# Last stage of a graph network with experts: expert outputs one step later, reciprocal roots on GpSimd, gate sums earlier, stores from SP's queue

## The chip, the cores and the metric

One core of one Trainium2 chip runs the whole program in one launch. The metric is the device time in microseconds (us) of that core, median over runs. Engines: PE is TensorE (PEld its weight loads), DVE is VectorE, ACT is ScalarE, POOL is GpSimd, SP is SyncE, which here only issues DMAs.

## The reference, cut to what matters

6250 nodes of 256 features, 206250 edges. An attention layer over the edges (all ahead of the last stage) leaves for every node a sum of weighted values and the sum of weights. What the last stage computes, for every node:

```python
out = weighted_values / (sum_of_weights + 1e-16)          # attention, by head
x_r = xn @ Wskip.T + bskip                                # xn: normalised x
beta = sigmoid(concat([out, x_r, out - x_r]) @ Wbeta.T)
h = beta * x_r + (1.0 - beta) * out
y = layernorm(xn + h, ln1_g, ln1_b)
t = layernorm(y + gelu(y @ W1.T + b1) @ W2.T + b2, ln2_g, ln2_b)
x2 = x + t
m = layernorm(x2)                                         # no gain, no bias
shared = relu(relu(m @ sW1 + sb1) @ sW2 + sb2) @ sW3 + sb3
expert[e] = relu(relu(m @ eW1[e] + eb1[e]) @ eW2[e] + eb2[e]) @ eW3[e] + eb3[e]   # 4 experts
gates = softmax(m @ gW + gb); w = softmax(top-2 of gates)
result = x2 + shared + sum(w[e] * expert[e])
```

All is float32. W1 is 256 to 1024, sW1 256 to 256, sW2 256 to 128, eW1 256 to 128, eW2 128 to 64, eW3 64 to 256.

## The kernel before, in words

Two stages come first and are not touched: normalisation with the key, value and query products, and the attention over the edges. The last stage begins at about 3006 us of the span. It works on the 49 blocks of 128 nodes in 13 parts (`parts`, `wd`): the first of 3 blocks, eleven of 4, the last of 2. Each engine has its own hand-written program, and they meet at semaphores only. Matrix operands are kept feature-major, so row tiles are transposed by TensorE (`transpose_rows`, L1440) into two buffers `tr`, and copied out by ScalarE (`transposed`, L1364). `r0` are the transposes of xn, `r1` of y, `r2` of m. Hidden layers (`hidden`, L1449 on TensorE, L1387 on ScalarE) go through two PSUM buffers `hid`: `w1` has 8 groups of four matmuls, `s1` 2, `e1` 4, `s2` 1, `e2` 4. Products that come out by node (`node_major`, L1456) go through three PSUM buffers `nat`: `skip` (two matmul pairs a block), `w2` (8 pairs a block) and `out` (one tile for the shared branch and one for each expert, so five tiles a block, each read by VectorE). A float32 product of 256 columns shows as two matmuls in the trace. For `nat` and `hid` a list `order` gives every tile its number; the same order must hold on the engine that fills and the one that empties.

A step s works on part s with W1 and W2 and on part c = s - 1 with the experts. TensorE's order in a step: W1(s), with the transposes of m(c) after its fifth group, gate logits (L1482), s1(c), W2(s), e1(c), s2(c), e2(c), transposes of y(s+1) and xn(s+2), expert outputs of c, skip(s+2).

VectorE's order in a step: `after_attention(s+1)` (gate sum L1236 to L1239, gate L1241 to L1245, first layer norm, y; L1256 is its last line), `gates(c)`, `divide_by_sum(s+2)` (L1215 to L1219), `add_ffn(s)` (L1264), `after_ffn(s)` (second and third layer norm; the last gives `mb`, which is m), `combine(c)` (L1323 and L1328, reading the output tiles), `skip_less_out(s+2)` (L1227). Every layer norm (`layernorm`) takes statistics (L1200), seven short operations (L37 to L43), waits for ScalarE's reciprocal root and scales (L1207).

ScalarE computes the root as exp(-0.5 ln(var + eps)) in `rstd`, L1376 and L1378, at three places of a step, and the gates' exponentials (L1369, L1382). Changing between these functions and gelu makes it load a table.

SP's queue loads weights, then for each step xn(s+3) and x(s+1); GpSimd's queue stores each part (L1170, L1173) once it is combined.

Of the kernel before, what the change touches and what calls it, by code (L numbers as in the profile page):

```python
# [24 lines left out]
ALU = mybir.AluOpType  # L25
ACT = mybir.ActivationFunctionType
AX = mybir.AxisListType

P = 128
# [16 lines left out]
def build(nc, a, out):  # L46
# [75 lines left out]
    with top:  # L122
# [877 lines left out]
        with ExitStack() as s3:  # L1000

            W = 4
# [42 lines left out]
            eps3 = sbt(s3, "eps3", [P, 1])  # L1047
# [5 lines left out]
            lv3 = sbt(s3, "lv3", [P, W])  # L1053
            rs3 = sbt(s3, "rs3", [P, W])
            zb = sbt(s3, "zb", [P, W])
# [33 lines left out]
            ws_landed, w3_landed, consts3, rows_set = sem("ws_landed"), sem("w3_landed"), sem("consts3"), sem("rows_set")  # L1089
# [10 lines left out]
            with nc.Block() as block:  # L1100
                @block.sync
                def _(sp):
# [39 lines left out]

                    for dst, src in loads[:NW3S]:
                        sp.dma_start(dst, src).then_inc(ws_landed, 16)
# [6 lines left out]
                    for s in range(NS):  # L1151
                        if s + 3 < NS:
                            load_xn(s + 3)
                        if s + 1 < NS:
                            load_x(s + 1)

                @block.gpsimd
                def _(pool):
                    pool.memset(tri[:, :, :], 1.0).then_inc(consts3, 1)
                    pool.wait_ge(consts3, 1)  # L1160

                    pool.affine_select(out=tri[:, :, :], in_=tri[:, :, :], compare_op=ALU.is_ge, fill=0.0, base=-1,
                                       pattern=[[1, NE], [-1, NE]], channel_multiplier=0).then_inc(consts3, 1)

                    for p, (t0, t1) in enumerate(parts):
                        pool.wait_ge(out_ready, p + 1)
                        whole = min(t1, N // P) - t0
                        last = min(t1 * P, N) - (t0 + whole) * P
                        if whole:
                            pool.dma_start(out[t0 * P:(t0 + whole) * P, :].rearrange("(j p) d -> p j d", p=P), accb[:, 0:whole, :]  # L1170
                                           ).then_inc(out_stored, 16)
                        if last:
                            pool.dma_start(out[(t0 + whole) * P:N, :], accb[0:last, whole, :]).then_inc(out_stored, 16)  # L1173
                    pool.wait_ge(out_stored, 16 * (NS - 1 + (whole > 0) + (last > 0)))

                @block.vector
                def _(dve):
                    ch = Chain(dve, "dve3")

                    dve.memset(eps3[:, :], LN_EPS).then_inc(rows_set, 1)  # L1180
# [17 lines left out]
                    def layernorm(dst, src, w):  # L1198
                        for j in range(w):
                            s = dve.bn_stats(st3[:, j, :], src[:, j, :])  # L1200
                        ch.step(s)
                        mean_and_var(dve, ch, st3[:, 0:w, :], mn3[:, 0:w], vr3[:, 0:w], D)
                        dve.sem_inc(var_ready, 1)
                        lns[0] += 1
                        dve.wait_ge(rstd_ready, 2 * lns[0])
# [24 lines left out]
                    def after_attention(p):  # L1230

                        w, d = wd[p], db[p % 3]
                        ob, x, t, y = weighted(p)[:, :, :, 0:C], xnb[p % 2], ta[:, 0:w, :], yb[:, 0:w, :]
# [5 lines left out]
                        dve.tensor_reduce(zb[:, 0:w], t, AX.X, ALU.add).then_inc(z_ready, 1)  # L1239
                        dve.wait_ge(ez_ready, p + 1)  # L1240
# [94 lines left out]
                    skip_less_out(0)  # L1335
                    after_attention(0)
                    divide_by_sum(1)
                    skip_less_out(1)
                    for s in range(NS + 1):
                        if s + 1 < NS:  # L1340
                            after_attention(s + 1)
                        if s >= 1:
                            gates(s - 1)
                        if s + 2 < NS:
                            divide_by_sum(s + 2)
                        if s < NS:
                            add_ffn(s)
                            after_ffn(s)
                        if s >= 1:
                            combine(s - 1)  # L1350
                        if s + 2 < NS:
                            skip_less_out(s + 2)

                @block.scalar
                def _(act):
                    act.wait_ge(rows_set, 2)
                    lns = [0]
# [13 lines left out]
                    def rstd(p):  # L1371

                        w = slice(0, wd[p])
                        lns[0] += 1
                        act.wait_ge(var_ready, lns[0])
                        act.activation(lv3[:, w], vr3[:, w], ACT.Ln, bias=eps3[:, 0:1]).then_inc(rstd_ready, 1)  # L1376
                        act.wait_ge(rstd_ready, 2 * lns[0] - 1)
                        act.activation(rs3[:, w], lv3[:, w], ACT.Exp, scale=-0.5).then_inc(rstd_ready, 1)  # L1378

# [9 lines left out]
                    transposed(0, 0)  # L1389
                    transposed(0, 1)  # L1390
                    exp_z(0)
                    rstd(0)
                    transposed(1, 0)
                    act.wait_ge(w3_landed, 16 * (NW3 - NW3S))
                    for s in range(NS + 1):
                        c = s - 1
                        if s < NS:
                            for k in range(KH):
                                hidden("w1", s, k, h1, ACT.Gelu, b1c)
                                if k == 2 and s + 1 < NS:  # L1400
                                    exp_z(s + 1)
                                if k == 4 and c >= 0:
                                    transposed(2, c)
                                if k == 5 and s + 1 < NS:
                                    rstd(s + 1)
                        elif c >= 0:
                            transposed(2, c)
                        if c >= 0:
                            for k in range(KD):
                                hidden("s1", c, k, sh1, ACT.Relu, sb1c)  # L1410
                            exp_gates(c, 0)
# [8 lines left out]
                        elif s < NS:  # L1420
                            rstd(s)
                        if s + 1 < NS:
                            transposed(1, s + 1)
                        if s + 2 < NS:
                            transposed(0, s + 2)
                        if s < NS:
                            rstd(s)

                @block.tensor
                def _(pe):  # L1430
                    pe.wait_ge(ws_landed, 16 * NW3S)
                    pe.wait_ge(rows_set, 2)
# [59 lines left out]
                    for s in range(NS + 1):  # L1492
                        c = s - 1
# [7 lines left out]
                        elif c >= 0:  # L1501
                            rows_of_m(c)
                        if c >= 0:
                            wc = wd[c] * P
                            gate_logits(c)
                            for k in range(KD):
                                hidden("s1", c, k, P, [(sW1[:, i, k * P:(k + 1) * P], rT[2][:, i, 0:wc]) for i in range(KD)])
                        if s < NS:
# [3 lines left out]
                        if c >= 0:  # L1512
# [7 lines left out]
                        if s + 1 < NS:  # L1520
                            rows_of_y(s + 1)
                        if s + 2 < NS:
                            rows_of_x(s + 2)
                        if c >= 0:
                            pe.wait_ge(hid_emptied, hid_at["e2", c] + NE)
                            for j in range(wd[c]):
                                cols, n = slice(j * P, (j + 1) * P), nat_at["out", c] + j * (1 + NE)
                                node_major(n, [(sh2[:, cols], sW3[:, :])])
                                for e in range(NE):
                                    node_major(n + 1 + e, [(e2[:, e, cols], eW3[:, e, :])])  # L1530
                        if s + 2 < NS:
                            skip(s + 2)
# [59 lines left out]
```

## Time and profile before

| what | value |
|---|---|
| median of 3 runs | 4067.2 us (4065.84 to 4069.83) |
| the profiled execution's own time | 4068.84 us |
| its span in the trace | 4067.0 us |
| mean granted clock of TensorE | 0.952 |
| busy over the span: TensorE, VectorE, ScalarE, GpSimd | 91%, 48%, 41%, 50% |

The profile is one execution recorded on the chip. Busy time is that of instructions at work; a wait is idle time with the engine or queue whose event ended it. The granted clock is given as a share of 2.4 GHz, so 0.50 is 1.2 GHz. The page cuts the span into 40 slices of about 102 us; the last stage fills slices 31 to 40. In the rows below, times are microseconds from the span's start.

### The profile page before, as it was taken

What the parts mean: (1) busy time and instruction counts of PE and PEld (TensorE: products, weight loads), DVE (VectorE), ACT (ScalarE), POOL (GpSimd) and SP (SyncE); (2) the same over time, 40 slices, a digit from 0 to 9 for tenths busy, and PEclk for the clock granted to TensorE, in tenths of its full rate; (3) what the DMA queues carried; (4) which work ended last, traced back from release to release, by engine and by line L of the source; (5) the groups of instructions that cost most, each with busy time, mean ns of one, the idle gap of its engine ahead of it and who ended that gap; (6) DMA issues with size and microseconds to landing.
All of it is one profiled execution on the core that took longest, in us unless ns stands there. A gap on an engine that the chain in (4) does not pass through costs nothing. (4 is left out here: it accounts for less than half of the span.)

```text
span 4067.0 us, 77637 instructions
## 1 busy us (share of the span) xinstructions
PE 3700.7 (91%) x22914; PEld 2352.3 (58%) x22914; DVE 1970.6 (48%) x5552; ACT 1681.0 (41%) x3636; POOL 2046.7 (50%) x2100
## 2 busy tenths in 40 slices
PE   5879999999999999999999999999967888888888
PEld 2346666666666666666666666666645555555555
DVE  5344444444444444444444444444446555555544
ACT  2134444444444444444444444444424343433442
POOL 3067777777777777777777777777720000000000
PEclk9989999999999999999999999999988888888887
DMA  6467677776777767777776777767740000000000
GB/s 200 156 164 186 181 184 184 189 186 183 185 185 186 187 184 187 186 185 189 187 190 183 185 188 186 182 183 190 188 105 21 15 26 16 21 16 22 13 13 13
DMA packets 637776, 572.41 MB, mean 141 GB/s; under 512 B 430486, under 2 KB 523991, under 8 KB 637700
## 3 DMA queue, kind: packets, MB, share of 16 engines
q0 software_dynamic: 159616, 429.57, 35.9%
q1 hardware_dynamic: 478100, 142.10, 16.8%
q8 instruction: 30, 0.49, 0.1%
q14 instruction: 30, 0.25, 0.0%
HBM read 632.99 MB, written 33.05 MB: 164 GB/s over the span
## 5 line engine op out<-in xcount | busy, mean ns | idle before, releaser
L610 POOL DMA_INDIRECT F<-kv_rows,srcg x1970 | 1994.7, 1013 | 841.2 <-issue 564.4
L688 DVE COPY PT<-pPT 128x384 f32<-128x384 f32 x393 | 219.0, 557 | 1164.9 <-PE pPT L878 1146.4
L885 PE MATMUL pZ<-F,PT 128*64 128x320 f32 x4704 | 743.1, 434 | 0.0
L858 PE MATMUL ring<-ident,F 128*128 128x128 f32 x3940 | 605.8, 285 | 120.6 <-ACT FT L790 111.9
L858 PEld LDWEIGHTS ring<-ident,F 128*128 128x128 f32 x3940 | 420.3, 141 | 406.4 <-ACT FT L790 203.9
L796 ACT ACTIVATE Pw<-pS,nMn 128x384 f32<-128x384 f32 x393 | 226.8, 577 | 954.5 <-DVE nMn L683 954.5
L790 ACT ACTIVATE FT<-ring 128x512 f32<-128x512 f32 (+1 forms) x1182 | 579.1, 525 | 73.4 <-PE ring L858 10.4
L1170 POOL DMA_DIRECT2D out_dram<-accb x13 | 9.7, 749 | 1047.1 <-DVEq L1332 1047.1
L885 PEld LDWEIGHTS pZ<-F,PT 128*64 128x64 f32 x4704 | 366.4, 136 | 254.5 <-issue 0.5
L867 PE MATMUL pS<-FT,qh 128*64 128x320 f32 x3144 | 512.0, 447 | 1.5 <-issue 1.1
L682 DVE TENSOR_REDUCE nmx<-pS 128x1 f32<-128x384 f32 x393 | 219.2, 558 | 202.1 <-PE pS L871 200.5
L867 PEld LDWEIGHTS pS<-FT,qh 128*64 128x64 f32 x3144 | 191.2, 136 | 157.9 <-issue 2.5
L871 PE MATMUL pS<-F,G 80*64 80x320 f32 x1572 | 279.7, 433 | 0.0
L834 ACT ACTIVATE Zs<-pZ 128x320 f32<-128x320 f32 x392 | 171.6, 438 | 185.3 <-PE pZ L885 185.3
L1456 PE MATMUL nat<-eW,e 65*128 65x256 f32 x392 | 168.0, 598 | 63.2 <-DVE accb L1323 63.2
L676 DVE TENSOR_SCALAR F<-F,nid 16x640 f32<-16x640 int32 x394 | 214.4, 544 | 19.2 <-issue 1.3
L898 PE MATMUL pZv<-ident,Zs 128*128 128x64 f32 x1568 | 218.2, 262 | 0.0
L878 PE MATMUL pPT<-ident,Pw 128*128 128x128 f32 x1179 | 215.3, 291 | 1.1 <-ACT Pw L796 1.1
L891 PE MATMUL pM<-ident,F 64*128 64x64 f32 x1965 | 206.6, 233 | 0.0
L898 PEld LDWEIGHTS pZv<-ident,Zs 128*128 128x128 f32 x1568 | 205.9, 192 | 0.0
L808 ACT ACTIVATE G<-pM 64x512 f32<-64x512 f32 x99 | 58.5, 591 | 352.4 <-PE pM L848 352.4
L891 PEld LDWEIGHTS pM<-ident,F 64*128 64x128 f32 x1965 | 153.0, 139 | 66.2 <-issue 66.2
(215 smaller groups left out, 4458.0 us busy)
## 6 DMA issues: line engine op xcount, KB each, us to landing
F<-in_edge_attrT SPq DMA_DIRECT2D x788, 80.0 KB
F<-kv_rows,srcg POOLq DMA_INDIRECT x1970
F<-in_dst SPq DMA_DIRECT2D x788, 20.0 KB
srci<-src_front SPq DMA_DIRECT2D x796, 1.5 KB, 3.5
kv_rows<-kvs SPq DMA_DIRECT2D x7, 1792.0 KB, 6.7
qb<-q_cols SPq DMA_DIRECT2D x100, 64.0 KB, 2.9
U<-in_x SPq DMA_DIRECT2D x7, 896.0 KB, 10.9
xn_rows<-xs SPq DMA_DIRECT2D x7, 896.0 KB, 6.7
```

Of the source, the lines that this page charges most:

```text
L610: pool.indirect_dma_start(out=F[s][:, t, 0:KV], out_offset=None, in_=kv_d, in_offset=bass.IndirectOffsetOnAxis(ap=srcg[j % GB][:, col:col ...
L682: ch.step(dve.tensor_reduce(nmx[:, j:j + 1], pS[:, 0:SW], AX.X, ALU.max, negate=True))
L688: dve.tensor_copy(PT[:, :, :], pPT[:, 0:SW].rearrange("p (t r) -> p t r", r=P)).then_inc(pt_emptied, 1)
L790: act.activation(FT[j % 2][:, :, t0 * P:t1 * P], ring[n % 2][:, 0:KD * w].rearrange("p (k e) -> p k e", e=w), ACT.Copy).then_inc(ring_empt ...
L796: act.activation(Pw[:, :], pS[:, 0:SW], ACT.Exp, bias=nMn[:, j:j + 1], accum_out=lsum[:, j:j + 1]).then_inc(p_done, 1)
L858: m = pe.transpose(ring[n % 2][:, k * w + (t - t0) * P:k * w + (t - t0 + 1) * P], F[j][:, t, k * P:(k + 1) * P], ident[:, :])
L867: pe.matmul(pS[o * HP:(o + 1) * HP, o * HP:o * HP + OW], qh[half][:, c, g + o, :, :].rearrange("p c r -> p (c r)"), FT[j % 2][:, c, o * OW ...
L871: m = pe.matmul(pS[o * HP:(o + 1) * HP, o * HP:o * HP + OW], G3[half][0:K3, g + o, :, :].rearrange("p c r -> p (c r)"), F3[s][0:K3, o * OW ...
L878: m = pe.transpose(pPT[:, t * P:(t + 1) * P], Pw[:, t * P:(t + 1) * P], ident[:, :])
L885: m = pe.matmul(pZ[rows, 0:ZW], PT[:, t, rows], F[s][:, o * TO + t, D:FP], start=(t == 0), stop=(t == KB - 1))
L891: m = pe.transpose(pM[:, t * DE:(t + 1) * DE], F3[s][0:DE, t * P:(t + 1) * P], ident[0:DE, 0:DE])
L898: pe.matmul(pZv[:, g].rearrange("p (o c r) -> p o c r", o=2, c=KD)[:, :, c, :], Zs[:, c * P:(c + 1) * P], ident[:, :].rearrange("p (o c r) ...
```

## The change

Four things change, all in the last stage.

- The expert outputs and `combine` of a part move one step later. TensorE's order in a step becomes: W1(s) with the transposes of m(s-1), expert outputs of s - 2, gate logits and s1(s-1), transposes of y(s+1) and xn(s+2), W2(s), skip(s+2), e1, s2, e2(s-1). There is one step more, and `order` follows.
- The reciprocal root becomes one power, (var + eps) to -0.5, on GpSimd, with eps added by VectorE. GpSimd sets a constant of -0.5 at the start.
- The gate's wide sum (`gate_sum`) leaves `after_attention(p)` and runs two steps earlier in VectorE's text, after `skip_less_out(p)` in the step before; the exponential for it comes at the end of ScalarE's step.
- The stores are issued from SP's queue.

```diff
-            for s in range(NS + 1):
-                order += [("w1", s), ("r2", s - 1), ("s1", s - 1), ("w2", s), ("e1", s - 1), ("s2", s - 1), ("e2", s - 1),
-                          ("r1", s + 1), ("r0", s + 2), ("out", s - 1), ("skip", s + 2)]
+            for s in range(NS + 2):
+                order += [("w1", s), ("r2", s - 1), ("out", s - 2), ("s1", s - 1), ("r1", s + 1), ("r0", s + 2), ("w2", s),
+                          ("skip", s + 2), ("e1", s - 1), ("s2", s - 1), ("e2", s - 1)]
...
                 @block.sync
-                    for s in range(NS):
+                    for s in range(NS + 2):
                         if s + 3 < NS:
                             load_xn(s + 3)
+                        if s >= 2:
+                            store(s - 2)
                         if s + 1 < NS:
                             load_x(s + 1)
+                    sp.wait_ge(out_stored, 16 * stored[0])
...
                 @block.gpsimd
+                    pool.memset(half[:, :], -0.5).then_inc(half_set, 1)
...
+                    def rstd(p):
+                        lns[0] += 1
+                        pool.wait_ge(var_ready, lns[0])
+                        pool.tensor_tensor(rs3[:, 0:wd[p]], vr3[:, 0:wd[p]], half[:, 0:wd[p]], ALU.pow).then_inc(rstd_ready, 1)
...
                 @block.vector
+                        ch.step(dve.tensor_scalar(vr3[:, 0:w], vr3[:, 0:w], LN_EPS, None, ALU.add))
                         dve.sem_inc(var_ready, 1)
...
-                    for s in range(NS + 1):
+                    for s in range(NS + 2):
                         if s + 1 < NS:
                             after_attention(s + 1)
-                        if s >= 1:
+                        if s >= 2:
+                            combine(s - 2)
+                        if 1 <= s <= NS:
                             gates(s - 1)
                         if s + 2 < NS:
                             divide_by_sum(s + 2)
                         if s < NS:
                             add_ffn(s)
-                            after_ffn(s)
-                        if s >= 1:
-                            combine(s - 1)
                         if s + 2 < NS:
                             skip_less_out(s + 2)
+                            gate_sum(s + 2)
+                        if s < NS:
+                            after_ffn(s)
...
                 @block.scalar
-                                if k == 2 and s + 1 < NS:
-                                    exp_z(s + 1)
-                                if k == 5 and s + 1 < NS:
-                                    rstd(s + 1)
...
+                        if s + 1 < NS:
+                            transposed(1, s + 1)
+                        if s + 2 < NS:
+                            transposed(0, s + 2)
                         if c >= 0:
                             exp_gates(c, 0)
                             exp_gates(c, 1)
                             for e in range(NE):
                                 hidden("e1", c, e, e1, ACT.Relu, eb1c)
-                                if e == 1 and s < NS:
-                                    rstd(s)
                             hidden("s2", c, 0, sh2[:, None, :], ACT.Relu, sb2c)
                             for e in range(NE):
                                 hidden("e2", c, e, e2, ACT.Relu, eb2c, EH2)
...
+                            exp_z(s + 2)
...
                 @block.tensor
-                    for s in range(NS + 1):
-                        c = s - 1
+                    for s in range(NS + 2):
+                        c, o = s - 1, s - 2
...
+                        if o >= 0:
+                            pe.wait_ge(hid_emptied, hid_at["e2", o] + NE)
+                            for j in range(wd[o]):
+                                cols, n = slice(j * P, (j + 1) * P), nat_at["out", o] + j * (1 + NE)
+                                node_major(n, [(sh2[:, cols], sW3[:, :])])
+                                for e in range(NE):
+                                    node_major(n + 1 + e, [(e2[:, e, cols], eW3[:, e, :])])
```

## Rows read from the trace of the kernel before

**Rows 1.** Busy time by stretch: PE, PEld, DVE, ACT, POOL, PEclk, DMA share, GB/s.
```profile
3647.60:3729.60 82.00, 72.28 (x229) 45.85 (x229) 47.70 (x115) 32.59 (x51) 0.75 (x1) 0.85 0.06 20
```
**Rows 2.** Chain of waits that ended last: start us, us, what.
```profile
3155.47 1.39 DVE mb L1207 x4
...
3808.35 1.39 DVE mb L1207 x4
...
3889.36 1.39 DVE mb L1207 x4
...
3965.55 1.39 DVE mb L1207 x4
```
**Rows 3.** Timeline of PE: start us, us, engine line op, shapes, count [idle before <-releaser].
```profile
3565.74 2.08 PE L1456 MATMUL nat<-eW,e 65*128 65x256 f32 x4 [5.43 <-DVE accb L1323]
...
3585.55 8.75 PE L1449 MATMUL hid<-rT,W1T 128*128 128x512 f32 x20
...
3604.34 5.35 PE L1449 MATMUL hid<-rT,sW 128*128 128x512 f32 x8 [0.79 <-ACT h L1387]
3609.53 13.98 PE L1456 MATMUL nat<-W2T,h 128*128 128x256 f32 x64
...
3631.51 1.96 PE L1449 MATMUL hid<-sh,sW 128*128 128x512 f32 x4 [1.14 <-ACT e L1387]
...
3637.22 0.66 PE L1440 MATMUL tr<-ident,yb 128*128 128x128 f32 x4
...
3640.22 0.71 PE L1440 MATMUL tr<-ident,xnb 128*128 128x128 f32 x4 [0.26 <-ACT rT L1364]
```
**Rows 4.** Busy time in stretches of 2 us, columns as in rows 1.
```profile
3563.70:3565.70 2.00, 0.00 (x0) 0.00 (x0) 1.91 (x3) 0.15 (x1) 0.00 (x0) 0.50 0.00 0
...
3577.70:3579.70 2.00, 2.00 (x6) 1.55 (x6) 0.97 (x2) 0.00 (x0) 0.00 (x0) 0.50 0.00 0
...
3605.70:3607.70 2.00, 2.00 (x3) 0.67 (x2) 1.93 (x3) 0.00 (x0) 0.00 (x0) 0.50 0.00 0
```
**Rows 5.** Timeline of DVE, first step and a full step, columns as in rows 3.
```profile
3096.24 1.06 DVE L1207 TENSOR_SCALAR mb<-tb,mn,rs 128x256 f32<-128x256 f32 x3 [1.94 <-ACT rs L1378]
...
3586.20 1.22 DVE L1236 TENSOR_TENSOR ta<-U,w 128x1024 f32<-128x1024 f32 x1
...
3593.14 0.17 DVE L1241 TENSOR_SCALAR ezb<-ezb 128x4 f32<-128x4 f32 x1 [1.93 <-ACT ezb L1369]
...
3602.33 1.38 DVE L1207 TENSOR_SCALAR db<-ta,mn,rs 128x256 f32<-128x256 f32 x4 [2.89 <-ACT rs L1378]
...
3607.52 0.17 DVE L1286 TENSOR_TENSOR g<-pg,rows 128x16 f32<-128x16 f32 x1
...
3624.00 1.41 DVE L1200 BATCH_NORM_STATS2 st<-tb 128x6 f32<-128x256 f32 x4
...
3630.83 1.38 DVE L1207 TENSOR_SCALAR db<-tb,mn,rs 128x256 f32<-128x256 f32 x4 [4.02 <-ACT rs L1378]
...
3644.51 1.38 DVE L1207 TENSOR_SCALAR mb<-tb,mn,rs 128x256 f32<-128x256 f32 x4 [5.57 <-ACT rs L1378]
```
**Rows 6.** Timeline of POOL in the first stage, columns as in rows 3.
```profile
59.87 4.52 POOL L283 TENSOR_SCALAR_AFFINE_SELECT selh<-selh 128x4 f32<-128x4 f32 x14
...
91.26 1.64 POOL L315 MEMSET U<- 128x1848 f32 x1 [3.79 <-DVE xs L354]
```
**Rows 7.** Timelines of PE and DVE at the end, columns as in rows 3.
```profile
4025.34 2.08 PE L1456 MATMUL nat<-eW,e 65*128 65x256 f32 x4 [3.52 <-DVE accb L1323]
...
4041.54 1.87 PE L1482 MATMUL pg<-gW,rT 128*128 128x4 f32 x8 [0.47 <-ACT rT L1364]
...
4046.82 2.49 PE L1449 MATMUL hid<-rT,eW 128*128 128x256 f32 x8
...
4057.90 2.04 DVE L1328 SCALAR_TENSOR_TENSOR accb<-nat,we,accb 128x256 f32<-128x256 f32 x4
```
**Rows 8.** DMA issues of the last stage: count, KB each, median us to landing.
```profile
out_dram<-accb POOLq DMA_DIRECT2D x11, 512.0 KB, 3.3
```

More of the change, by code:

```diff
@@ L1052, in build @@
             vr3 = sbt(s3, "vr3", [P, W])
-            lv3 = sbt(s3, "lv3", [P, W])
             rs3 = sbt(s3, "rs3", [P, W])
+            half = sbt(s3, "half", [P, W])
             zb = sbt(s3, "zb", [P, W])
@@ L1141, in load_x, with store @@
                         sp.dma_start(xb[:, 0:t1 - t0, :], x_d[:, t0:t1, :]).then_inc(xb_landed, 16)
+                    stored = [0]
+                    def store(p):
+                        t0, t1 = parts[p]
+                        sp.wait_ge(out_ready, p + 1)
+                        whole = min(t1, N // P) - t0
+                        last = min(t1 * P, N) - (t0 + whole) * P
+                        if whole:
+                            stored[0] += 1
+                            sp.dma_start(out[t0 * P:(t0 + whole) * P, :].rearrange("(j p) d -> p j d", p=P), accb[:, 0:whole, :]
+                                         ).then_inc(out_stored, 16)
+                        if last:
+                            stored[0] += 1
+                            sp.dma_start(out[(t0 + whole) * P:N, :], accb[0:last, whole, :]).then_inc(out_stored, 16)
                     for dst, src in loads[:NW3S]:
@@ L1160, in _ @@
                     pool.wait_ge(consts3, 1)
+                    pool.memset(half[:, :], -0.5).then_inc(half_set, 1)
+                    pool.wait_ge(half_set, 1)
                     pool.affine_select(out=tri[:, :, :], in_=tri[:, :, :], compare_op=ALU.is_ge, fill=0.0, base=-1,
                                        pattern=[[1, NE], [-1, NE]], channel_multiplier=0).then_inc(consts3, 1)
[L1165 to L1174, printed above, removed]
+                    lns = [0]
+                    def rstd(p):
+                        lns[0] += 1
+                        pool.wait_ge(var_ready, lns[0])
+                        pool.tensor_tensor(rs3[:, 0:wd[p]], vr3[:, 0:wd[p]], half[:, 0:wd[p]], ALU.pow).then_inc(rstd_ready, 1)
+                    rstd(0)
+                    for s in range(NS):
+                        if s + 1 < NS:
+                            rstd(s + 1)
+                        rstd(s)
+                        rstd(s)
                 @block.vector
@@ L1239, in after_attention @@
                         dve.tensor_reduce(zb[:, 0:w], t, AX.X, ALU.add).then_inc(z_ready, 1)
+                        dve.wait_ge(z_ready, p + 1)
+                    def after_attention(p):
+                        w, d = wd[p], db[p % 3]
+                        ob, x, t, y = weighted(p)[:, :, :, 0:C], xnb[p % 2], ta[:, 0:w, :], yb[:, 0:w, :]
                         dve.wait_ge(ez_ready, p + 1)
@@ L1335, in _ @@
                     skip_less_out(0)
+                    gate_sum(0)
                     after_attention(0)
@@ L1511, in _ @@
                                 node_major(nat_at["w2", s] + j, [(h1[:, k, j * P:(j + 1) * P], W2T[:, k, :]) for k in range(KH)])
-                        if c >= 0:
+                        if s + 2 < NS:
+                            skip(s + 2)
+                        if 0 <= c < NS:
                             for e in range(NE):
@@ L1519, in _ @@
                                 hidden("e2", c, e, EH2, [(eW2[:, e, :], e1[:, e, 0:wc])])
[L1520 to L1532, printed above, removed]
 NW3, NW3S = 26, 10
```

47 lines of the change are left out of this document (19 added, 28 removed).

## The prediction

> **What bounds the kernel now.** I read the page first: TensorE is the only engine near full, and slices 31 to 40, the last stage, differ from the rest: GpSimd idles and TensorE's clock drops. Only that stage is changed; I price nothing ahead of 3010 us. Next came the busy times by stretch. One step (a part of four blocks) takes 82 us: TensorE 72.3 us busy at a mean granted clock of 0.85, VectorE 47.7, ScalarE 32.6 [rows 1]. No engine is full; order and clock set the step. The chain of waits shows the ring. I mark a part c by its "mb", the last normalisation (call its end M(c)): M(1) = 3156.9, M(9) = 3809.7, so (3809.7 - 3156.9)/8 = 81.6 us a part; M(10) = 3890.7, M(11) = 3966.9 [rows 2]. TensorE's timeline has the holes. After the first tiles of "out" it stands 5.43 us, until VectorE has finished mb and can combine; two more holes are 0.79 us and 1.14 us, behind ScalarE [rows 3]. The fine stretches give the larger cost: after the hole the clock is 0.50 (1.2 GHz) and stays there through all expert outputs, with TensorE busy 2.00 of 2.00 us; it is 0.50 once more behind the gate logits [rows 4]. Expert outputs and skip thus take 19.8 us (3565.74 to 3585.55) [rows 3]. VectorE waits 2.89, 4.02 and 5.57 us for ScalarE's reciprocal roots [rows 5].
>
> **The change, part by part.**
> *Roots on GpSimd.* Log, exponential and their table loads leave ScalarE; VectorE gets one small addition (0.20 us with its gap, like its neighbours), GpSimd one power of 128x4, called p with both hand-offs. The trace has no power on GpSimd. Below: a chained small selection, 14 in 4.52 us, 0.32 us each; above: its longest computing row, 1.64 us for 128x1848 [rows 6]. The operand has four columns, so I take a value near the low end, p = 0.6, and keep both. Three a part.
> The Trainium skill ("GPSIMD Engine Reference", 4.1 Engine selection) speaks against the move: elementwise work belongs on VectorE, GpSimd being about twice as slow on two inputs. No row tests that; it would put p at an estimated 0.4 us and change the sum by some 8 us.
>
> *Gate sums early.* The four wide passes move from ahead of the gate's exponential to behind skip's subtraction, in the previous step. They are 5.0 us (3586.20 to 3593.14 less the wait of 1.93) [rows 5], still on VectorE's way, now ahead of mb instead of behind it; the wait for that exponential goes.
>
> *Expert outputs a step later.* Combine(s-2) now stands behind after_attention(s+1), and outputs(s-2) behind W1(s). Does VectorE come to it before TensorE? Count both from the end of skip. TensorE: e1, 16 matmuls at 0.43 us (20 in 8.75) = 6.9; s2 and e2, 3631.51 to 3637.22 = 5.7; W1's first five groups 8.6; rows_of_m 2.0 (four tiles through two buffers, my estimate); W1's last 12 matmuls 5.2; three output tiles (as many as there are buffers) 1.3 [rows 3]. Sum 29.7 us.
> VectorE: last subtraction 0.7; gate sum 5.0; after_ffn up to mb, 2.8 + 0.2 + p + 8.1 + 0.2 + p + 1.4 = 12.7 + 2p (3624.00 to 3630.83 less 4.02; 3630.83 to 3644.51 less 5.57; mb itself) [rows 5]; bias addition 1.26; after_attention without its sum, 6.3 + 0.2 + p + 5.2 = 11.7 + p (3593.14 to 3602.33 less 2.89; 3602.33 to 3607.52) [rows 5]; first release 0.45. Sum 31.8 + 3p = 33.6. **So TensorE still waits, about 4 us**, at the same door. In this trace holes of 5.43 and 3.52 us were followed by half clock, those of 1.14 and 0.79 us in themselves were not [rows 3, 7]. I expect the clock to fall again, and outputs never raised it [rows 4].
>
> *The new ring.* mb, bias 1.26, after_attention 11.7 + p, outputs 0.45 + 17 tiles at 0.854 (two matmuls of 0.43 each at half clock; VectorE needs only 0.51 a tile, four in 2.04 [rows 7]) = 14.9, gate logits at half clock 3.7 (eight take 1.87 [rows 7]), s1 partly at half clock 6.0 (between 5.35 [rows 3] and 8 x 0.86), transposes of y and x 3.6 (3637.22 to 3640.9, [rows 3]), W2 13.8, skip 3.5 (a quarter of W2's matmuls), subtraction 0.7, gate sum 5.0, after_ffn 12.7 + 2p: 76.9 + 3p = **78.7 us** against 81.6 on average before [rows 2]. The rest of TensorE (e1, s2, e2, W1) lies beside VectorE; if that cover were gone it would cost the 1.6 us between 21.2 (TensorE's arrival at rows_of_m) and 18.4 + 2p (mb).
>
> *First steps.* Ahead of M(0) come transposes 3.6, skip 3.5, 0.7 and gate sum 5.0, less about 7 us of root and exponential waits: M(0) = 3097.3 [rows 5] + 6 = 3103. M(1): 1.3 + 10.5 + p + 3.6 + 13.8 + 3.5 + 0.7 + 5.0 + 12.7 + 2p = 53, so 3156, as before. M(2): ring less five tiles, 74.4. M(9) = 3156 + 74.4 + 7 x 78.7 = 3781, 28 us early. M(10): skip, gate sum and transposes of a two-block part, 4.8 less, 73.9: 3855, 36 early.
> *Last steps.* Here the new order has least against it. M(11): no skip, no gate sum, a short after_attention (9.3 with p), so the hole shrinks to about 1 us and the clock should hold: 9.3 + 8.6 + 1.8 + 5.4 + 1.0 + 13.8 + 0.7 + 13.9 = 54, against 76.2 (bias and after_attention; outputs at VectorE's pace; logits; s1; transposes of y; W2; subtraction; after_ffn). M(12): TensorE sets it, 2.3 + 1.9 + 2.6 + 9.6 + 1.8 + 4.4 + 6.9 + 0.7 + 9.5 = 40 (its lateness at rows_of_m, those transposes, W1's rest on two blocks, outputs, logits, s1, W2 on two blocks, subtraction, after_ffn on two blocks). From M(12) to the end 37: 2.4 more of e1 to e2 of part 11, transposes 1.0, outputs 9.6, logits 1.5, s1 2.5, and from part 12's e1 to the end as before, 4046.8 to 4067.0, 20.2 [rows 7]. That is 77 against 4067.0 - 3966.9 = 100. End 3855 + 54 + 77 = 3986, **81 us early**.
>
> *Stores from SP's queue.* 14 DMAs move. SP's order is next x-norm load, store, next x load; the load behind the store waits for x_used anyway, set later in the same step than out_ready, and combine of the next part asks for the store a step later. Cost nothing; if that cover were gone, one transfer, 3.3 us, a step [rows 8]. The final store stays behind the last combine.
>
> The profiled execution took 4068.8 us for a span of 4067.0, 1.6 us above the median of 4067.2. 4068.8 - 81 = 3988, less 1.6: **3986 us**. Anything within 0.2% (8 us) of 4067 counts as the same, about what measurements of this kernel tell apart.
>
> **Rivals.**
> 1. *The clock holds.* If the hole is nearer 2 us, outputs go at VectorE's pace: 0.45 + 8.2 instead of 14.9, logits 1.8 instead of 3.7, s1 3.5 to 5.4 instead of 6.0. The ring falls to about 68 to 70 us, 9.5 less, nine times: some 85 us, **3900 us**. For: ScalarE's two smaller holes go, and my 4 us is a difference of two sums near 30 that an error of 2 us would halve. Against: 31.8 - 29.7 leaves 2.1 us even at p = 0. Also in this case: the clock falls but rises during the outputs. The Trainium skill ("TensorE: Matmul & The Clock Gate", What's actually happening) says that busy stretches release the throttle. The trace disagrees for these matmuls of 65 rows: busy throughout at 0.50, without a rise [rows 4]. Chance 0.24.
> 2. *Slower: the power is dear.* 39 powers (13 x 3) stand one behind another on VectorE's way, so the time is 3986 + 39 (p - 0.6). It passes 4067 at p = 2.7; at p = 3.5 it is **4099 us**. For: no power in the trace, and each is a wait of VectorE with everything queued behind it. Against: the two bounds [rows 6]. Chance 0.07 of being slower; between p = 1.6 and 2.7 (4025 to 4067) another 0.05.
> 3. *Only the ring gains.* The last two stretches gain 22 and 23 us by my sum; if each hides a wait that I have not seen, and the clock falls there too, nearly all of it goes: **4030 us**. For: no full step precedes them, so their clock is the least certain. Chance 0.12.
> 4. *The change doesn't do what it says*: outputs wait for mb through VectorE's order all the same and the removed root waits come back elsewhere: **4067**. Chance 0.02.
>
> **How the numbers follow.** Forecast 0.50 for 3986, its own range 3960 to 4020. The range reaches down over rival 1 (3895) and up to part of rival 3 (4038), leaving out 0.15 to 0.2. Faster 0.91, same 0.02, slower 0.07.
>
> **What the profile after would show.** ScalarE's loads fall to two a step, roots gone; GpSimd shows 39 powers: their mean is the first thing to read. A step of 78 to 79 us; a hole of about 4 us before an output tile, ended by VectorE's accb, and 0.50 behind it until s1; M(11) - M(10) near 54. I am wrong if the hole is under 2 us or outputs run at 1.00 (rival 1), if VectorE's idle before L1207 exceeds 1.6 us (rival 2), or if TensorE waits for m instead.

## The result, and the profile after

The changed kernel took 3996.40 us (median of 3 runs, 3996.38 to 3996.52) against 4067.2 us: a ratio of 0.9825, 95% interval 0.9803 to 0.9847, 71 us off. 3986 us was predicted, with 3895 to 4038 as its range. In a later comparison it took 3999.59 us against 4066.54 us (0.9837, 0.9823 to 0.985).

In the profiled execution (span 3994.6 us) TensorE's last product of line 913, after which the last stage follows, starts at 3000.4 us, and at 3004.3 us in the profile before. I therefore also give the **last stage**, the span less that start: 1062.7 us before, 994.2 us after, a gain of 68.5 us. Where a time below is set beside one that the prediction forecast, 3.9 us are added to it.

First the chain of waits that ended last, over one part (start us, us, what), to be read against [rows 2]:

```profile
3643.79 0.44 DVE accb L1353
3644.27 14.87 PE nat L1473 x34
3659.14 3.21 PE pg L1499 x16
3662.35 5.40 PE hid L1466 x8
...
3671.38 17.28 PE nat L1473 x80
...
3692.93 1.23 DVE zb L1263
...
3697.33 1.02 POOL rs L1191
3698.38 1.39 DVE db L1231 x4
...
3706.84 1.02 POOL rs L1191
3707.88 1.39 DVE mb L1231 x4
...
3717.20 1.01 POOL rs L1191
3718.24 1.39 DVE db L1231 x4
```

This is the ring that the prediction drew: expert outputs, logits, s1, transposes, W2 with skip, gate sum, the LayerNorms, and round again, with three powers on it. TensorE's timeline of the same part, against [rows 3]:

```profile
3636.94 0.59 PE L1473 MATMUL nat<-sW,sh 128*128 128x256 f32 x2
3637.37 1.03 PE L1473 MATMUL nat<-eW,e 65*128 65x256 f32 x4
3644.27 2.07 PE L1473 MATMUL nat<-eW,e 65*128 65x256 f32 x4 [5.87 <-DVE accb L1353]
...
3651.26 3.62 PE L1473 MATMUL nat<-eW,e 65*128 65x256 f32 x8
...
3658.94 3.41 PE L1499 MATMUL pg<-gW,rT 128*128 128x4 f32 x16
3662.21 5.53 PE L1466 MATMUL hid<-rT,sW 128*128 128x512 f32 x8
```

Three output tiles go out at 1.03 us for four matmuls, then TensorE stands 5.87 us for VectorE's first release, and the same four matmuls take twice as long. The fine stretches, against [rows 4] (columns as in rows 1):

```profile
3642.00:3644.00 2.00, 0.00 (x0) 0.00 (x0) 1.93 (x3) 0.00 (x0) 0.00 (x0) 0.51 0.00 0
...
3650.00:3652.00 2.00, 2.00 (x6) 1.64 (x5) 1.26 (x3) 0.00 (x0) 0.00 (x0) 0.50 0.00 0
3662.00:3664.00 2.00, 2.00 (x4) 1.02 (x5) 0.52 (x3) 0.00 (x0) 0.00 (x0) 0.50 0.13 46
3672.00:3674.00 2.00, 2.00 (x11) 1.77 (x10) 0.53 (x4) 1.32 (x2) 0.00 (x0) 1.00 0.00 0
```

The granted clock is 0.50 (1.2 GHz) from the hole on into s1, with TensorE busy 2.00 of 2.00 us once the hole is over, and 1.00 in W2. VectorE's timeline shows why the release is late, against [rows 5]:

```profile
3628.23 1.38 DVE L1231 TENSOR_SCALAR mb<-tb,mn,rs 128x256 f32<-128x256 f32 x4 [1.18 <-POOL rs L1191]
...
3638.60 1.38 DVE L1231 TENSOR_SCALAR db<-ta,mn,rs 128x256 f32<-128x256 f32 x4 [1.18 <-POOL rs L1191]
...
3643.79 0.42 DVE L1353 TENSOR_TENSOR accb<-nat,tb 128x256 f32<-128x256 f32 x1
```

Attention's LayerNorm and y of the next part stand between mb and the first release. VectorE waits 1.18 us for each root in place of 2.89, 4.02 and 5.57 us. One row of the page has the powers:

```profile
L1191 POOL TENSOR_TENSOR rs<-vr,half 128x4 f32<-128x4 f32 (+2 forms) x39 | 37.9, 972 | 916.4 <-DVEq L1227 916.4
```

The end differs from the ring in the last parts. Ahead of the outputs shown next, VectorE has only the short attention of the two-block part to do, and after that none. TensorE's timeline there, the counterpart of [rows 7]:

```profile
3874.76 2.00 PE L1473 MATMUL nat<-eW,e 65*128 65x256 f32 x8
...
3883.83 1.84 PE L1499 MATMUL pg<-gW,rT 128*128 128x4 f32 x16
3885.54 3.68 PE L1466 MATMUL hid<-rT,sW 128*128 128x512 f32 x8
```

Without a hole ahead of them, eight output matmuls take 2.0 us, the logits 1.84 and s1 3.68, where the ring pays 3.62, 3.41 and 5.53.

### The profile page after: what moved, and what is told of

It reads as the page before. It is cut to its first block and busy times, and to the rows that moved or that the text cites. A ratio compares the mean times of both kernels' runs of the same rounds, so it can differ in the third digit from the quotient of the medians.

```text
span 3994.6 us, 77537 instructions
## 1 busy us (share of the span) xinstructions
PE 3671.7 (92%) x22914; PEld 2332.8 (58%) x22914; DVE 1977.5 (50%) x5590; ACT 1519.0 (38%) x3445; POOL 2073.7 (52%) x2126
## 5 line engine op out<-in xcount | busy, mean ns | idle before, releaser
L790 ACT ACTIVATE FT<-ring 128x512 f32<-128x512 f32 (+1 forms) x1182 | 578.8, 525 | 73.6 <-PE ring L858 10.4
L1191 POOL TENSOR_TENSOR rs<-vr,half 128x4 f32<-128x4 f32 (+2 forms) x39 | 37.9, 972 | 916.4 <-DVEq L1227 916.4
L1473 PE MATMUL nat<-eW,e 65*128 65x256 f32 x392 | 150.7, 547 | 51.8 <-DVE accb L1353 51.8
```

The source lines that it names most:

```text
L790: act.activation(FT[j % 2][:, :, t0 * P:t1 * P], ring[n % 2][:, 0:KD * w].rearrange("p (k e) -> p k e", e=w), ACT.Copy).then_inc(ring_empt ...
L1473: m = pe.matmul(nat[n % NATS][:, 0:D], l, r, start=(q == 0), stop=(q == len(terms) - 1))
```

## The experiments

Theory: the time of a part is set by the ring through VectorE, three powers long; TensorE's hole in it costs its own length and then the clock behind it. The question that the result left: are 71 us what the moved roots bring, or a rest of it, with the order of the outputs taking something back? Rivals: the reorder is the gain and the roots a detail; or the hole is harmless and the clock falls for another reason.

### Each half of the change alone

**Roots only**: the kernel before, with the roots as powers on GpSimd, everything else in its old place.

```diff
-                        dve.wait_ge(rstd_ready, 2 * lns[0])
+                        dve.wait_ge(rstd_ready, lns[0])
...
+                    def rstd(p):
+                        lns[0] += 1
+                        pool.wait_ge(var_ready, lns[0])
+                        pool.tensor_tensor(rs3[:, 0:wd[p]], vr3[:, 0:wd[p]], half[:, 0:wd[p]], ALU.pow).then_inc(rstd_ready, 1)
```

> The kernel before with its reciprocal roots alone moved to GpSimd; order of work, gate sums and stores stay as they were. Theory (the root waits kept VectorE late for the first output tile): from the end of W2, VectorE needs 0.6 + 12.7 + 2.4 + 1.3 + 0.4 = 17.4 us to its first release, TensorE 6.9 + 5.7 + 3.6 + 1.3 = 17.5 to the third tile, so the hole of 5.4 us closes, the clock stays at 1.00 and the outputs go at VectorE's 0.51 us a tile: a step of 67 to 70 us against 81.9, the whole near 3930 us, faster than the changed kernel. Rival 1 (the gain of the change is its order): the step falls only by the two root waits on the way to mb, about 7 us, the clock still drops: near 3990. Rival 2 (root waits lie beside other work): 4060 to 4067.

**Order only**: the changed kernel, with logarithm and exponential for the roots back on ScalarE, after W1's third and eighth groups and after e1. Other places for them on ScalarE were not tried, so its time holds for these places.

```diff
-                        pool.tensor_tensor(rs3[:, 0:wd[p]], vr3[:, 0:wd[p]], half[:, 0:wd[p]], ALU.pow).then_inc(rstd_ready, 1)
...
+                        act.activation(lv3[:, w], vr3[:, w], ACT.Ln, bias=eps3[:, 0:1]).then_inc(rstd_ready, 1)
+                        act.wait_ge(rstd_ready, 2 * lns[0] - 1)
+                        act.activation(rs3[:, w], lv3[:, w], ACT.Exp, scale=-0.5).then_inc(rstd_ready, 1)
```

> The changed kernel with its roots back on ScalarE (logarithm and exponential), placed after W1's third group, after its eighth and after e1; order, gate sums and stores as changed. Theory: every root costs 3.1 to 4 us instead of GpSimd's 1.4 with the added eps, all on the way of mb: a step of 86 to 90 us against 80.2, the steps lose against the kernel before and the last two parts gain, 4060 to 4110 us. Rival (the order is what brings the gain): at most 4010 us.

Measured on one chip, the kernel before at 4066.89 us (the changed kernel's time is that of the first comparison, beside 4067.2):

| | outputs as before | outputs a step later |
|---|---|---|
| roots on ScalarE | 4066.9 us | 4144.9 us (ratio 1.0187, 1.017 to 1.0204) |
| roots on GpSimd | 3882.7 us (0.9549, 0.9533 to 0.9565) | 3996.4 us (the changed kernel) |

The roots bring 184 us by themselves; the new order (with early gate sums and SP's stores) costs 78 us with slow roots and 114 us with fast ones (116 us on one chip, in the last table). The first came out 47 us below what was expected, the second 35 us above the range given: both expectations took the cost of the order too low. TensorE's timeline with the roots alone moved:

```profile
3591.99 0.60 PE L1455 MATMUL nat<-sW,sh 128*128 128x256 f32 x2
3592.42 2.24 PE L1455 MATMUL nat<-eW,e 65*128 65x256 f32 x8
...
3601.79 3.69 PE L1455 MATMUL nat<-WskT,rT 128*128 128x256 f32 x16
...
3615.78 0.71 PE L1439 MATMUL tr<-ident,mb 128*128 128x128 f32 x4 [1.28 <-ACT rT L1381]
```

and its busy time over one step (columns as in rows 1):

```profile
3568.90:3633.50 64.60, 62.32 (x230) 37.88 (x229) 47.91 (x117) 22.41 (x38) 3.84 (x4) 1.00 0.07 21
```

No hole ahead of the outputs, the clock at 1.00 throughout, and TensorE busy 62.32 of 64.60 us: a step is 17 us shorter than the 81.6 before. The reason lies in rows shown already. VectorE's root waits fall from 12.48 us to about 3.5, some 9 us less, and the hole that these waits caused was 5.43 us; so VectorE now comes to its combine in time. This holds for the steps of the ring; the clock falls once more near the end (see "Beyond both kernels"). With the order alone VectorE waits 4.76, 5.07 and 2.42 us for roots:

```profile
3705.19 1.38 DVE L1220 TENSOR_SCALAR mb<-tb,mn,rs 128x256 f32<-128x256 f32 x4 [4.76 <-ACT rs L1401]
3719.23 1.38 DVE L1220 TENSOR_SCALAR db<-ta,mn,rs 128x256 f32<-128x256 f32 x4 [5.07 <-ACT rs L1401]
...
3781.06 1.38 DVE L1220 TENSOR_SCALAR db<-tb,mn,rs 128x256 f32<-128x256 f32 x4 [2.42 <-ACT rs L1401]
3793.93 1.38 DVE L1220 TENSOR_SCALAR mb<-tb,mn,rs 128x256 f32<-128x256 f32 x4 [4.76 <-ACT rs L1401]
```

The step is 3793.93 - 3705.19 = 88.7 us, 8.4 above the 80.3 of the changed kernel (mean of seven steps); the waits are 12.25 - 3.54 = 8.7 us longer. In the new order nearly every microsecond of a root is on the ring.

### Each power twice

```diff
+                        pool.tensor_tensor(rs2[:, 0:wd[p]], vr3[:, 0:wd[p]], half[:, 0:wd[p]], ALU.pow)
                         pool.tensor_tensor(rs3[:, 0:wd[p]], vr3[:, 0:wd[p]], half[:, 0:wd[p]], ALU.pow).then_inc(rstd_ready, 1)
```

> The changed kernel with every power taken twice on GpSimd (the first into a tile that nobody reads). Theory (39 powers one behind another on VectorE's way): 39 times 1.0 us more, 4035 us, a step 3.0 us longer. Rival (the power is hidden, or the step is pinned by the clock): 3996 to 4010 us.

Measured: 4037.62 us (0.9929, 0.9912 to 0.9946), 41 us above the changed kernel. The last stages, 1031.6 and 994.2 us, differ by 37.4, or 0.96 for each of 39 powers: about a power's length, but not evenly. Each of VectorE's waits grows by 0.97 us, and the step from 80.3 to 82.8, so 2.5 us for three (3.0 expected). From M(10) to M(11) (M as in the prediction, the end of a part's mb) it is 65.4 us against 54.2, since a hole opens where the changed kernel has none, and the outputs behind it run at half speed:

```profile
3908.31 1.82 PE L1475 MATMUL nat<-eW,e 65*128 65x256 f32 x4 [1.76 <-DVE accb L1355]
...
3910.78 3.62 PE L1475 MATMUL nat<-eW,e 65*128 65x256 f32 x8
```

From M(11) to the end it is 3.7 us less. So the roots of a part lie almost wholly on the ring, and the agreement of the total with 39 full powers is in part luck.

### The hole filled with useless work

Twelve products that nobody reads, on TensorE ahead of the expert outputs of a part (of ten parts in the changed kernel), and the same in the kernel before (eleven parts):

```diff
+                        if o >= 0 and s + 1 < NS:
+                            for _ in range(12):
+                                pe.matmul(pg[:, 2 * P:4 * P], W2T[:, 0, 0:P], W2T[:, 1, 0:D], start=True, stop=True)
```

> The changed kernel, with 12 products of 128x256 (W2 by itself, written to an unused part of the gate logits' bank, read by nobody) put on TensorE ahead of each part's expert outputs, 5.2 us of useless work in a hole of 5.9 us. Theory (the hole drops the clock, the dropped clock costs 10 us a step): the outputs run at 1.00, a tile each 0.51 us, a step of 70 us against 80.2, about 3910 us, faster with more work. Rival (outputs are slow for another reason: their 65 rows, VectorE, the buffers): 3996 us, or later by what the filler overruns.

> The kernel before, with 12 products of 128x256 that nobody reads on TensorE ahead of a part's expert outputs, where it waits in every part of the ring. Nothing else is changed. Theory: what the wait costs is mostly the granted clock behind it (outputs, pg and logits at 0.50); with TensorE kept busy in the wait the clock holds, and a part takes some 73 to 74 us in place of 82: about 3965 us (3940 to 4000). Rival: the wait is what costs, the clock follows from something else: 4067 us or, with the products' own 1.5 us in each part, up to 4085 us.

Measured for the changed kernel with it: 3932.07 us (0.9665, 0.9648 to 0.9681). The step falls from 80.3 to 71.53 us. TensorE's timeline and the busy times by stretch show why:

```profile
3603.03 1.22 PE L1473 MATMUL nat<-eW,e 65*128 65x256 f32 x4 [0.66 <-DVE accb L1353]
```

```profile
3587.00:3658.53 71.53, 69.10 (x253) 43.09 (x252) 47.90 (x116) 19.86 (x36) 3.02 (x3) 0.98 0.07 23
...
3610.00:3612.00 2.00, 2.00 (x14) 1.77 (x14) 1.86 (x5) 0.00 (x0) 0.00 (x0) 1.00 0.00 0
```

VectorE is as late as before (from the end of mb to the matmul that it releases it is 14.7 us in both), but TensorE has worked until then, and the outputs run at 1.00. So of what the hole costs a part, 8.8 us are the clock behind it; the wait itself is still there, as useless work. The step was expected 1.5 us shorter and the time 22 us shorter (3910): s1 still takes 5.38 us in place of 3.68, since the clock is 0.50 again behind the logits (3615 to 3617 us).

The kernel before with the same products ran with three others on a second chip, on which the kernel before itself took 4753.19 us. The attention stage is slower there (the last product of line 913 starts at 3672 to 3704 us), while the last stage is not: one and the same kernel (roots and gate's exponential on GpSimd, below) has a last stage of 865.0 us there and of 863.9 us on another chip. I compare last stages. With the products it is 4670.8 - 3703.6 = 967.2 us against 1062.7, 95 us shorter (84 us by the medians on that chip, ratio 0.9821, 0.9791 to 0.9852), 73.1 us a step on average:

```profile
4289.96:4364.00 74.04, 69.57 (x254) 42.98 (x253) 47.40 (x113) 32.57 (x52) 0.75 (x1) 0.98 0.07 22
4364.00:4436.36 72.36, 67.89 (x254) 42.41 (x253) 47.41 (x114) 32.58 (x52) 0.75 (x1) 1.00 0.06 19
```

Useless products alone give the kernel before more than the 68.5 us that the change gives in the last stage. The wait's own length was the smaller part of its price, in both kernels.

### The order on VectorE, and the old places restored

**Combine first**: in the changed kernel VectorE takes the combine of part s-2 ahead of attention's LayerNorm of part s+1.

```diff
-                        if s + 1 < NS:
-                            after_attention(s + 1)
                         if s >= 2:
                             combine(s - 2)
+                        if s + 1 < NS:
+                            after_attention(s + 1)
```

> The changed kernel with one move on VectorE: the combine of part s-2 is issued ahead of the attention's LayerNorm and y of part s+1. Theory: TensorE's wait ahead of the expert outputs (5.87 us) goes, since it is for VectorE's adds that queue behind that LayerNorm; in its place TensorE waits for y behind the skip product, some 7 us, with the clock falling there; about 73 us for a part and 3930 us. Rival: the new wait costs as much as the old, 80 us for a part, 3996 us or more.

Measured: ratio 0.9742 (0.9717 to 0.9767), last stage 4608.3 - 3672.0 = 936.3 us, 58 less than the changed kernel's, 72.9 us a step. The hole has moved, as expected:

```profile
4218.21 2.28 PE L1457 MATMUL tr<-ident,yb 128*128 128x128 f32 x8 [7.37 <-DVE yb L1284]
```

It is longer than the old one (7.37 against 5.87 us) and yet costs less, since what follows it is 16 transposes and W2 in place of thirty-odd output matmuls, sixteen logits and s1: W2's 64 matmuls take 14.10 us, against 13.98 in the changed kernel, so the clock is back by then. The clock over a step is 0.93 to 0.95, against 0.83 and 0.85.

**Old places**: the changed kernel with outputs, skip, combine and the transposes of y and xn where they were (and the gate's exponential back behind W1's third group); roots on GpSimd, gate sum early and stores from SP's queue stay.

```diff
-            for s in range(NS + 2):
-                order += [("w1", s), ("r2", s - 1), ("out", s - 2), ("s1", s - 1), ("r1", s + 1), ("r0", s + 2), ("w2", s),
-                          ("skip", s + 2), ("e1", s - 1), ("s2", s - 1), ("e2", s - 1)]
+            for s in range(NS + 1):
+                order += [("w1", s), ("r2", s - 1), ("s1", s - 1), ("w2", s), ("e1", s - 1), ("s2", s - 1), ("e2", s - 1),
+                          ("r1", s + 1), ("r0", s + 2), ("out", s - 1), ("skip", s + 2)]
```

> The changed kernel, but with the expert outputs, the skip product and VectorE's combine back in the places that they had before (outputs of a part behind its own W2, ahead of the next y and W1); the roots stay one power on GpSimd, the gate sum stays right behind the LayerNorm, and the stores stay on SP's queue. Theory: the whole loss against the kernel with the roots alone moved (3882.7 us) is the order of the outputs, and gate sums and SP's stores are worth nothing: 3883 us, within 10, a part of the ring each 64.6 us, TensorE's clock at 1.00. Rival: the early gate sum puts itself ahead of VectorE's work for y or for the combine, or SP's stores hold the loads: 3900 to 3990 us.

Measured: ratio 0.9613 (0.959 to 0.9636) on the second chip, last stage 874.5 us, 64.59 us a step, as with the roots alone. The new place of the outputs, with what moved along with it, is thus the whole of the loss. Early gate sums and SP's stores make 3 us at most, between 877.4 and 874.5, and not evenly: up to M(0) it is 4.7 us more than with the roots alone, from M(10) to M(11) 7.6 us less (62.9 against 70.5), where with the roots alone the clock falls, as shown below. The first of these was not looked into.

### Beyond both kernels

**Roots and the gate's exponential on GpSimd**, in the kernel before (w12 and w23 with their signs turned, so that zb is -z):

```diff
-                    def exp_z(p):
-                        act.wait_ge(z_ready, p + 1)
-                        act.activation(ezb[:, 0:wd[p]], zb[:, 0:wd[p]], ACT.Exp, scale=-1.0).then_inc(ez_ready, 1)
+                    def exp_z(p):
+                        pool.wait_ge(z_ready, p + 1)
+                        pool.tensor_tensor(ezb[:, 0:wd[p]], ec3[:, 0:wd[p]], zb[:, 0:wd[p]], ALU.pow).then_inc(ez_ready, 1)
```

> The kernel before with its roots on GpSimd (as in the run with the roots alone), and the gate's exponential made on GpSimd too, as e to the power of -z, so that ScalarE loads no table in the ring at all. The order of the outputs is that of before. Theory: the 1.28 us that TensorE still waits for ScalarE's rows of the transposes in each part goes, as ScalarE's two remaining loads were in its way: 63.2 to 63.6 us in place of 64.6 for each part, 3865 us (3855 to 3876). Rival: the wait has another releaser and stays, or GpSimd's power of the gate comes later than ScalarE's exponential did: 3883 us or somewhat above.

Measured on the second chip: ratio 0.9598 (0.9557 to 0.9639), last stage 865.0 us, 63.93 us a step. The expectation said that ScalarE then loads no table at all; that was careless, as the exponentials of the expert gates stay there. Loads fall from four a part to two. The last comparison put the versions side by side on a chip like the first, together with one that has all parts of the change but the new place of the outputs, and the gate's exponential on GpSimd:

> The changed kernel unaltered, beside the next three on one chip. Theory and rival alike: from TensorE's last product of line 913 to the end 994 us as in its first profile; the total follows from how long the stage before lasts on this chip: 3996 us, or some 4670 us where the granted clock of the attention stage is about 0.9.

> The kernel before with its roots on GpSimd and nothing else, unaltered, on the same chip as the changed kernel. Theory: 117 us less than the changed kernel from the last product of line 913 to the end (877 us), and some 114 us less in all: the order of the outputs costs that. Rival: the two chips so far differed, and the distance is smaller than 80 us.

> The kernel before with roots and the gate's exponential on GpSimd, unaltered. Theory: 0.65 us less for each part than with the roots alone, 12 us less in all: the ratio to it 0.997. Rival: no difference, since the wait for the rows of the transposes is made up elsewhere.

> The changed kernel with the outputs back in the places that they had before, and the gate's exponential on GpSimd as well as the roots; gate sum early, stores on SP's queue. Theory: what the parts give adds up: 3 us for the early start of the first part, 12 us for the gate's exponential: 862 us behind the last product of line 913, some 15 us less in all than with the roots alone. Rival: with the gate sum early its power on GpSimd stands in front of nothing, and the gain is that of the exponential alone, 865 us.

| | median of 5, us | ratio, 95% interval | last stage, us |
|---|---|---|---|
| changed kernel | 3999.59 | 0.9837, 0.9823 to 0.985 | 993.9 |
| roots alone | 3883.82 | 0.9549, 0.9536 to 0.9562 | 878.3 |
| roots and gate's exponential | 3871.05 | 0.9522, 0.9509 to 0.9535 | 863.9 |
| all parts, outputs in their old place | 3869.42 | 0.9513, 0.95 to 0.9526 | 864.4 |

(The kernel before: 4066.54, median of 9.) TensorE's waits in the last stage, in all, times and longest, first with the roots alone, then with the gate's exponential moved as well:

```profile
PE tr L1439 <- ACT rT L1381: 25.2, 45, 1.3
PE nat L1455 <- DVE db L1245: 23.9, 2, 15.0
PE tr L1439 <- DMA xnb<-xn_rows: 16.0, 1, 16.0
```

```profile
PE nat L1458 <- DVE db L1255: 24.6, 2, 15.7
PE tr L1442 <- ACT rT L1391: 17.9, 45, 0.6
PE tr L1442 <- DMA xnb<-xn_rows: 15.9, 1, 15.9
```

The longest wait for ScalarE's rows falls from 1.3 to 0.6 us, all of them from 25.2 to 17.9, and the time by 12.8 us, 12 expected. That the total agrees is luck. The last stage is 14.4 us shorter, and of that the parts from M(1) to M(10) give 5.0 (64.6 against 63.9 a step), while 8.3 lie between M(10) and M(11), 70.5 against 62.2. There the clock falls with the roots alone and holds with the exponential moved, behind holes of the same length (first the former, then the latter):

```profile
3728.06 1.22 PE L1455 MATMUL nat<-eW,e 65*128 65x256 f32 x4 [0.96 <-DVE accb L1341]
...
3729.74 3.66 PE L1455 MATMUL nat<-eW,e 65*128 65x256 f32 x8
```

```profile
3721.27 1.22 PE L1458 MATMUL nat<-eW,e 65*128 65x256 f32 x4 [0.96 <-DVE accb L1351]
...
3722.85 2.07 PE L1458 MATMUL nat<-eW,e 65*128 65x256 f32 x8
```

Why it falls in one of them stays open.

The two fastest can't be told apart: 1.6 us, intervals that overlap, last stages of 863.9 and 864.4; the 3 us that the early gate sum was thought to add are not seen. "ScalarE: Activation LUTs" of the Trainium skill (What ACT_TABLE_LOAD costs) puts a switch at 1.28 us of load and 1.38 of drain; the changed kernel's trace agrees on the load, but shows no drain: the instruction ahead of the load ends at 3671.80 us, and the one behind it comes at once:

```profile
3671.82 1.28 ACT L1406 ACT_TABLE_LOAD   x1
3673.12 0.21 ACT L1406 ACTIVATE gx<-g 128x16 f32<-128x16 f32 x1
```

What is left of waits in these two is mostly single long ones: 15.9 us for an x-norm load, and two for skip differences, 24.6 us in all.

## Why the prediction was right, and what it missed

**The forecast case happened, by its mechanism.** The order of the race at the outputs was counted as 31.8 + 3p against 29.7 us from the end of skip. Skip ends 79.65 us (a step) ahead of 3688.66, at 3609.0: VectorE's release comes 35.3 us later, TensorE 29.4 us later. The clock fell behind the hole and stayed down through the outputs; rivals 1 (it holds), 3 (only the ring gains) and 4 didn't happen.

**The term that was mis-sized is p.** "A value near the low end, p = 0.6": the trace has 1.18 us from the end of VectorE's addition to the normalisation, of which 1.01 is the power itself. By the prediction's own sums, 31.8 + 3 x 1.18 - 29.7 = 5.6 us of hole (measured 5.87, forecast about 4), and 76.9 + 3 x 1.18 = 80.4 us of ring (measured 80.3 on average from M(2) to M(9), forecast 78.7). The nearest-row argument failed: a selection on few columns says little of a power on few columns. The bounds of 0.3 and 1.6 us held. Doubling the powers showed the slope, 0.96 us on average for each of 39, so that rival 2 was a matter of size alone.

**The sum by stretches.** Two rows of the chain of waits give M(1) and M(9), with the length of mb and 3.9 us added:

```profile
3151.48 1.39 DVE mb L1231 x4
...
3788.65 1.39 DVE mb L1231 x4
```

M(0) was forecast at 3103 and came at 3102.7, M(1) at 3156 and 3156.8; here the dearer p was made up by other terms of the start. Eight steps later M(9) came at 3793.9, 12.9 us behind the forecast 3781, and 8 x 3 x 0.58 = 13.9. From there on the delay stays: M(10) is 75 us further (forecast 74), M(11) 54 (54), M(12) 39 (40), the end 37 (37). "Here the new order has least against it" held: no hole, outputs at 1.00. Of the ring's terms the outputs were exact (14.87 against 14.9), the logits a little high (3.2 against 3.7), s1 right on average (5.4 us in this part and 6.5 in the one before it, against 6.0), W2 and skip 17.28 against 17.3.

The last stage thus ended 12.5 us later than forecast, and the time came out 10.4 us later, 3996.4 against 3986: the stages ahead, which the change doesn't touch, happened to be 3.9 us shorter in this run, while the 1.6 us that the prediction took off, because the profiled execution of the kernel before was that much above its median, had no counterpart here. The gain that was priced at 81 us is 68.5. The formula of rival 2, 3986 + 39 (p - 0.6), gives 4009 with p = 1.18, too much: of the 39 powers the 24 from M(1) to M(9) show in the end.

**The side terms.** Two loads a part, as forecast. The gate sum of a part runs one step earlier than before, as the prediction has it (the description of the change says two). Stores from SP's queue and early gate sums were costed at nothing beyond what the ring already holds; with the outputs restored to their old place neither is seen in the time.

**The rule on engine selection** of the Trainium skill ("GPSIMD Engine Reference", 4.1 Engine selection), which gives elementwise adds, products and maxima to VectorE, points the wrong way for this operation in this place: GpSimd takes 1.01 us where VectorE's neighbouring operations (not powers) take 0.17, more than twice as slow, and yet the move is the whole gain, since it replaces waits of 2.9 to 5.6 us. A power on VectorE was not tried.

**What it missed** is the larger lesson, though no number on record depended on it. It priced the change as a whole, and not its parts against each other. The rows for "roots alone" were there: root waits of 12.48 us in a step, three of p in their place, so about 9 us less on VectorE ahead of a combine that was 5.43 us late. The hole closes, the clock stays up, and with 7.4 us of holes and the half clock behind them gone a step is 64.6 us. It took the hole that the reorder leaves (2.1 us even at p = 0) as an item of the sum, where it is the reorder's own doing: with combine behind attention's LayerNorm of a full part, VectorE can't win the race at any p.

## What to carry to other kernels

Price each part of a change alone against the rows, above all a reorder beside a removal: here the removal was worth 184 us and the reorder took 114 of them back. Count a wait of TensorE as its length plus what runs at half clock behind it, and ask what that is: a hole of 7.4 us ahead of transposes and W2 cost less than one of 5.9 ahead of the small output matmuls. If a hole can't be closed, useless products in it are a quick test of how much of its price is the clock.

## What the runs showed of the hardware

- GpSimd's power of two small operands: 1.01 us for 128x4, and 0.70 us for 128x2. Four columns take nearly as long as a wide pass on VectorE (1.22 us for 128x1024).
- Output matmuls of 65 rows don't bring TensorE's clock from 0.50 to 1.00 in some 15 us of busy time, but mostly hold it at 1.00 if they start there (2.07 us for eight of them, in the kernel with the roots alone). In that same kernel it once fell to 0.50 after the first of them had run at 1.00, behind a hole of 0.96 us.
- Twelve useless products in each of ten or eleven parts made both kernels faster, by 1.6% (3996.4 to 3932.1 us) and 1.8% (4753.2 to 4668.7 us).
- On one of the chips the stages ahead of the last took 670 to 700 us longer, with a mean granted clock of 0.91 for the span in place of 0.98 (roots and gate's exponential), while the last stage took 865.0 us there and 863.9 us elsewhere. What differs there stays open.
